# Placing the q/k projections of a recurrent-plus-MoE kernel inside its shared-expert loop

## The reference, cut to what matters

```python
q = xn @ Wq + bq;  k = xn @ Wk + bk;  v = xn @ Wv + bv     # 256 -> 256 each
logits = xn @ gate_w.T                                      # 16 experts, top 4, weights
# per expert: gather its tokens, silu(gate) * up, down; scatter-add with the weights
```

## Time and profile before

| what | value |
|---|---|
| median of 3 runs | 2452.93 us (2451.85 to 2453.05) |
| profiled execution, its own time | 2453.34 us |
| span of its profile | 2451.6 us |
| instructions in the profile | 38962 |
| `middle`, by the timeline | from about 1620 us to 1871 us |
| PE busy over the span | 2187.4 us (89%) |
| DVE, ACT, POOL busy | 1847.8, 1154.6, 1224.6 us |

### The profile page before, as it was taken

How to read it: one execution, slowest core, us unless ns; L and a number is a source line. 1 busy time by engine, 2 the same in 40 slices (tenths; PEclk the granted TensorE clock), 3 DMA queues, 4 the chain that set the end, 5 groups by cost and what they waited for, 6 DMA issues and landing times. The chain is left out here.

```text
span 2451.6 us, 38962 instructions
## 1 busy us (share of the span) xinstructions
PE 2187.4 (89%) x12914; PEld 1686.0 (69%) x12914; DVE 1847.8 (75%) x3389; ACT 1154.6 (47%) x2420; POOL 1224.6 (50%) x1324
## 2 busy tenths in 40 slices
PE   4995899999999999999999999968857998899982
PEld 3784688888888888888888888847755776344432
DVE  4885788888888888888888888744943444888746
ACT  1332455555555555555555555523333333366660
POOL 3544266565665665665656655533224332999000
PEclk9997699999999999999999999978988999799996
DMA  2002000000000000000000000043024555333214
GB/s 93 1 14 76 32 3 3 33 3 32 4 3 33 3 3 33 3 3 33 3 33 3 3 3 3 3 154 138 1 66 142 175 176 146 110 121 120 78 59 161
DMA packets 76743, 128.90 MB, mean 53 GB/s; under 512 B 22315, under 2 KB 54539, under 8 KB 74539
## 3 DMA queue, kind: packets, MB, share of 16 engines
q1 hardware_dynamic: 69584, 104.76, 12.5%
q0 software_dynamic: 6864, 18.75, 3.1%
q10 hardware_dynamic: 99, 2.88, 0.6%
HBM read 91.82 MB, written 46.92 MB: 57 GB/s over the span
## 5 line engine op out<-in xcount | busy, mean ns | idle before, releaser
L957 DVE SCALAR_TENSOR_TENSOR mix_cv<-mix_pp,mix_cw,mix_cv 128x384 f32<-128x384 f32 (+4 forms) x864 | 492.7, 570 | 25.4 <-ACT mix_cv L880 4.6
L804 PEld LDWEIGHTS mix_pyd<-mix_xdt,mix_lm 128*128 128x128 f32 x2048 | 248.4, 192 | 56.8 <-issue 53.1
L880 ACT ACTIVATE mix_cv<-mix_pp,mix_cb,mix_cw 128x384 f32<-128x384 f32 (+1 forms) x288 | 182.4, 633 | 205.1 <-PE mix_pp L80 205.1
L78 PE MATMUL mix_pp<-l0in_XH,mix_wx_lo 128*128 128x384 f32 (+2 forms) x576 | 239.1, 415 | 40.4 <-DVE mix_ss L946 25.4
L743 POOL TENSOR_TENSOR mix_xdt<-mix_xtok,l_dt 128x512 f32<-128x512 f32 x128 | 133.8, 1045 | 279.1 <-ACT mix_xtok L907 279.1
L736 POOL TENSOR_TENSOR mix_t<-mix_t,mix_xd 128x512 f32<-128x512 f32 x112 | 144.5, 1290 | 218.8 <-DVE mix_t L971 155.3
L855 PE MATMUL mix_pgt<-mix_wo,mix_gt 128*128 128x256 f32 x1024 | 246.4, 384 | 2.9 <-issue 2.2
L804 PE MATMUL mix_pyd<-mix_xdt,mix_lm 128*128 128x64 f32 x2048 | 243.7, 272 | 2.6 <-DVE mix_lm L1007 2.6
L1897 DVE TENSOR_REDUCE att_tops<-att_psc 128x1 f32<-128x512 f32 (+3 forms) x384 | 189.5, 549 | 47.3 <-PE att_psc L1845 32.2
L886 ACT ACTIVATE mix_pp<-mix_cv 128x384 f32<-128x384 f32 (+1 forms) x288 | 132.9, 462 | 161.7 <-DVE mix_cv L957 159.4
L855 PEld LDWEIGHTS mix_pgt<-mix_wo,mix_gt 128*128 128x128 f32 x1024 | 185.0, 191 | 31.5 <-issue 9.2
(11 more groups left out here) (382 smaller groups left out, 5817.5 us busy)
## 6 DMA issues: line engine op xcount, KB each, us to landing
mix_w_raw<-in_w_in SPq DMA_DIRECT2D x8, 1280.0 KB, 6.0
y_d<-exp_ys SPq DMA_DIRECT2D x79, 128.0 KB, 1.7
a_part<-att_sums SPq DMA_DIRECT2D x32, 256.0 KB, 5.0
mix_ll<-cs SPq DMA_DIRECT2D x384, 4.0 KB
q<-q SPq DMA_DIRECT2D x12, 512.0 KB, 4.5
k<-k SPq DMA_DIRECT2D x12, 512.0 KB, 4.5
att_qs<-q SPq DMA_DIRECT2D x32, 192.0 KB
att_ks<-k SPq DMA_DIRECT2D x32, 192.0 KB
```

The source lines that it names most:

```text
L78: pe.matmul(out, l_lo, r_hi, start=start, stop=False)
L804: last = pe.matmul(pyd[:, h * HP:(h + 1) * HP], lm[p % 2][:, h, :], xdt[p % 2][:, h * HP:(h + 1) * HP], start=True, stop=True)
L880: act.activation(conv_tile(k), pp[k % 2][:, halo:cols], ACT.Identity, bias=cb[:, it // 2, ct:ct + 1], scale=cw[:, it // 2, ct, 3:4]).then_ ...
L957: last = dve.scalar_tensor_tensor(out, of, cw[:, g, ct, 3 - d:4 - d], out, ALU.mult, ALU.add)
```

## The change

It moves the 16 q/k units into the loop over the shared expert's units. At n = 9 to 24 PE does, after the gate and up products of n, the projection of u = n-9, into the one bank `px`, and then the down product of n-2. The rest of unit u follows: high part on ACT at iteration n, after `hh`; DVE's subtraction at the head of iteration n+1; middle part (ACT) and low part (POOL) at n+1. The loops of ACT, DVE and POOL get the two more iterations that PE's has. Before the projection of u PE waits for DVE's subtraction of u-1.

The other parts: the output bank `po` is emptied behind `hh` of the same iteration (m = n-2, where it was m = n-3 ahead of it); token transposes, normalisations, logits, the prefix and the casts come one iteration later; q/k/v weights get buffers of their own and are split at n = 4 to 7; 28 matmuls of identity on identity are put ahead of PE's first transpose; the one-hot tables are made by 8 `tensor_tensor` compares of 16 columns' worth each (16x128 or 16x80 elements) in place of 128 `tensor_scalar` ones; `same` and `val` are made in two halves in one buffer, and the inversion is 32 matmuls at the head of n = 23 and 32 at the head of n = 25, summed in bank `pr`; the v tiles come after the loop, in banks `pg[0]` and `pu[0]`; the down weights are loaded by SP after the last q/k store has landed, and `experts` waits for them at its first down product (`w2_ld`); the table `keep` is loaded on its own.

```diff
-        DONE_AT = (0,) * 9 + (3, 9, 15, 21, 27, 32, 39, 42, 48, 50, 52, 54, 56, 57, 60, 60, 60) + (62,) * 14
-        PREFIX_AT, IDX_AT = 15, 2
+        TURN_AT = {4: 2, 5: 3, 6: 4, 7: 5, 8: 6, 9: 7}
+        NORM_AT = {3: 1, 5: 2, 7: 3}
+        LOGIT_AT = {0: 0, 6: 1, 8: 2, 10: 3}
+        DONE_AT = (0,) * 10 + (3, 9, 15, 21, 27, 32, 39, 42, 48, 50, 52, 54, 55, 57, 58, 61)
+        PREFIX_AT, IDX_AT = 16, (23, 25)
+        QK_AT, WARM = 9, 28
...
+                for a, sem in enumerate(stored):
+                    sp.wait_ge(sem, 16 * len(range(a, 16, NR3)))
+                sp.wait_ge(h_done, NU)
+                sp.wait_ge(idx_done, 2)
+                sp.wait_ge(dv, 61)
+                sp.dma_start(W[0:EI // 2, WG_COLS:], wd_d).then_inc(w2_ld, 16)
...
+                def third(u):
+                    pool.wait_ge(p1_done, u + 1)
+                    pool.tensor_tensor(part[u % NR3][:, 2, :], r, part[u % NR3][:, 1, :], ALU.subtract).then_inc(p2_done, 1)
...
+                def invert(half):
+                    pe.wait_ge(dv, (55, 58)[half])
+                    pe.wait_ge(val_done, half + 1)
+                    for j in range(NH2):
+                        last = pe.matmul(pr[:, 0:2 * TILE_COLS], opos[:, half * NH2 + j, :], val[:, j, :, :].rearrange("p v q -> p (v q)"),
+                                         start=half == 0 and j == 0, stop=half == 1 and j == NH2 - 1)
+                    last.then_inc(idx_done, 1)
...
+                for _ in range(WARM):
+                    pe.matmul(px[:, 0:P], ident[:, :], ident[:, :], start=True, stop=True)
...
+                    if n in IDX_AT:
+                        invert(IDX_AT.index(n))
...
                         last.then_inc(gu_done, 1)
+                    if 0 <= n - QK_AT < len(QK):
+                        project(n - QK_AT)
                     m = n - LAG
...
+                def second(u):
+                    act.wait_ge(sub1, u + 1)
+                    act.activation(part[u % NR3][:, 1, :], r, ACT.Copy).then_inc(p1_done, 1)
...
+                    if QK_AT < n:
+                        second(n - QK_AT - 1)
...
+                        act.wait_ge(h_done, n + 1)
+                        wait(act, out_done, n - NH + 1)
+                        act.activation(hh[n % NH][:, :], h[n % 2][:, :], ACT.Copy).then_inc(hh_done, 1)
+                    if 0 <= n - QK_AT < len(QK):
+                        u = n - QK_AT
+                        act.wait_ge(mm, u + 1)
+                        wait(act, stored[u % NR3], 16 * (u // NR3))
+                        col = u // 8 * 2 + u // 4 % 2
+                        act.activation(part[u % NR3][:, 0, :], px[:, :], ACT.Identity, bias=bq[:, col:col + 1]).then_inc(p0_done, 1)
+                    m = n - LAG
                     if m >= 0 and m % NS == NS - 1:
...
+                    if n in (22, 24):
+                        half = n // 2 - 11
+                        act.wait_ge(dv, (54, 57)[half])
+                        wait(act, idx_done, half)
+                        for t in range(NT // 2):
+                            last = act.activation(val[:, 4 * t:4 * t + 4, 0, :], same[:, 4 * t:4 * t + 4, :], ACT.Copy,
+                                                  scale=float(half * NT // 2 + t))
                         last.then_inc(val_done, 1)
...
-                        for i in range((j - 48) * 16, (j - 47) * 16):
-                            last = dve.tensor_scalar(opos[:, i, :], iota[:, :], posf[:, i:i + 1], None, ALU.is_equal)
+                        at = slice((j - 48) * 16, (j - 47) * 16)
+                        last = dve.tensor_tensor(opos[:, at, :], posf[:, at].unsqueeze(2).to_broadcast([P, 16, P]),
+                                                 iota[:, :].unsqueeze(1).to_broadcast([P, 16, P]), ALU.is_equal)
...
+                for n in range(NU + LAG):
+                    if QK_AT < n:
+                        u = n - QK_AT - 1
+                        dve.wait_ge(p0_done, u + 1)
+                        wait(dve, p2_done, u)
+                        col = u // 8 * 2 + u // 4 % 2
+                        dve.scalar_tensor_tensor(r, px[:, :], bq[:, col:col + 1], part[u % NR3][:, 0, :],
+                                                 ALU.add, ALU.subtract).then_inc(sub1, 1)
...
+                dispatch(61)
+                dispatch(62)
+                dve.wait_ge(dv, 63)
...
-                        pe.wait_ge(w_ld, 32)
+                        pe.wait_ge(w_ld, 16)
...
+                        if e == 0:
+                            pe.wait_ge(w2_ld, 16)
```

More of the change, by code:

```diff
@@ L1064, in middle @@
[L1064 to L1068, removed]
@@ L1069, in middle, with at @@
-        before = W[0:1, B:B + SLOTS1 * E].rearrange("p (j e) -> p j e", e=E)
+        def at(a, n):
+            return W[:, B + a:B + a + n]
+        raw = at(0, 3072).rearrange("p (i b k n) -> p i b k n", i=NS, b=2, k=KD)
+        draw = at(3072, 1536).rearrange("p (i n) -> p i n", i=NS)
+        oh = at(0, 1024).rearrange("p (t k e) -> p t k e", t=NT, k=TOPK)
+        big = at(1024, 1024).rearrange("p (t k e) -> p t k e", t=NT, k=TOPK)
+        cnt, inc, base = (at(1024 + i * 256, 256).rearrange("p (e t) -> p e t", e=E) for i in range(3))
@@ new lines, in middle @@
+        lg, cur, aux = (at(2048 + i * 256, 256).rearrange("p (t e) -> p t e", e=E) for i in range(3))
+        keep = at(2816, 256)
+        mb = at(3072, 128).bitcast(BF16).rearrange("p (t e) -> p t e", e=E)
+        slotf = at(3200, 64)
+        tileu, posu = (at(3264 + i * 64, 64).bitcast(U32) for i in range(2))
+        tilef, posf = keyb[:, 0, :], keyb[:, 1, :]
+        NH2 = NPAIR // 2
+        same = at(0, 1280).bitcast(BF16).rearrange("p (j q) -> p j q", j=NH2)
+        val = at(1280, 2560).bitcast(BF16).rearrange("p (j v q) -> p j v q", j=NH2, v=2)
@@ L1071, in middle @@
+        before = W[0:1, B:B + SLOTS1 * E].rearrange("p (j e) -> p j e", e=E)
+        wq = at(4608, 1536).rearrange("p (k n) -> p k n", k=KD)
+        trif = at(6656, 256)
+        part = [at(4352 + o * 768, 768).bitcast(BF16).rearrange("p (k t) -> p k t", k=3) for o in range(NR3)]
+        r = at(6656, TB)
+        th = [at(7168 + a * TB, TB) for a in range(2)]
         XN = VN[:, 0:NT * D].rearrange("p (t d) -> p t d", t=NT)
@@ L1466, in dispatch @@
                         dve.wait_ge(pfx_done, 1)
+                        dve.wait_ge(k_ld, 16)
                         last = dve.tensor_copy(cnt, pr[:, 256:512].rearrange("p (t e) -> p e t", e=E))
                     elif j == 33:
-                        last = dve.tensor_tensor_scan(inc.rearrange("p e t -> p (e t)"), table(C_KEEP, 256),
+                        last = dve.tensor_tensor_scan(inc.rearrange("p e t -> p (e t)"), keep,
                                                       cnt.rearrange("p e t -> p (e t)"), 0.0, ALU.mult, ALU.add)
@@ L1550, in _ @@
                 tokens_lo(1)
-                for n in range(NU):
-                    o = n % 2
-                    dve.wait_ge(th_done, n + 1)
-                    wait(dve, hl_done, n - 1)
-                    dve.scalar_tensor_tensor(h[o][:, :], th[o][:, :], 1.0, pg[o][:, :], ALU.add, ALU.mult).then_inc(s_done, 1)
-                    dve.wait_ge(s_done, n + 1)
-                    dve.tensor_tensor(h[o][:, :], h[o][:, :], pu[o][:, :], ALU.mult).then_inc(h_done, 1)
-                    extra(n)
@@ new lines, in _ @@
+                dispatch(61)
+                dispatch(62)
+                dve.wait_ge(dv, 63)
+                dve.memset(V[:, :, :, DH:], 1.0).then_inc(ones_set, 1)
+                dve.wait_ge(ones_set, 1)
+                for t in range(NT):
+                    dve.wait_ge(mv, t + 1)
+                    kt, side = t % (NT // 2), t // (NT // 2)
+                    dve.tensor_tensor(V[:, side * H1:(side + 1) * H1, kt, 0:DH], pv[t % 2][:, 0:D].rearrange("p (h c) -> p h c", h=H1),
+                                      bvs[:, :].rearrange("p (h c) -> p h c", h=H1), ALU.add).then_inc(vs, 1)
@@ L2131, in lay_out @@
     moe[:, C_PCOL] = np.arange(P)
-    moe[:, C_KEEP:C_KEEP + E * NT] = (np.arange(E * NT) % NT != 0)
+    keep = np.tile((np.arange(E * NT) % NT != 0).astype(np.float32), (P, 1))
     moe[:, C_ONES:C_ONES + E] = 1
```

219 lines of the change are left out of this document (79 added, 140 removed).

## The result

The changed kernel takes 2422.69 us (median of 4 runs, 2420.62 to 2423.21) against 2452.54 for the kernel before beside it: ratio 0.9876, 95% interval 0.9863 to 0.989. That is 29.9 us less. The prediction was 2423.0, in a range of 2410 to 2437. The profiled execution took 2423.18 us for a span of 2421.4; the profile of before has 2451.6, so the two spans are 30.2 us apart.

What follows compares the result with a forecast made beforehand. PE was taken to idle under DVE's one-hots and behind q/k stores held by the down weights' load. Gains 12.0 (early units) + 20.9 (unit 9 on) - 2.5 (handover) = 30.4 us gave 2423, range 2410 to 2437.

Steps and rivals of the forecast that it cites:

- the handover: From the last v add to the experts: the first gather may wait for the down weights' load, 2.5 us lost (0 to 4.5).
- the warm matmuls: Ahead of PE's first transpose: 28 matmuls lift the clock for the first logits and unit 0, 3.9 us gained (0 to 4.7).
- First nine units: Start of `middle` up to unit 9: 12.0 us gained in sum, ends 5 and 16.
- The two waits for transposes: In the first nine units: transposes one unit later find their rows ready, 5.4 us gained, plus 3.3 for a half-clock stretch.
- The output bank: In the first nine units: emptied right behind the down product, not behind the next tanh, 1.9 us gained.
- POOL's sixth low part: In the first nine units: the sixth weight slice's low part, needed by unit 5, comes late, 2.5 us lost (1 to 4).
- Unit 9 to the end of the last v add: Second stretch of `middle`: 109.1 us of PE's work plus 24.4 and 3 makes 136.5, a gain of 20.9 (10 to 32).
- the rounds: From unit 9 on: `dispatch` rounds and later scalar steps on DVE delay the next projections, 6 us of waits.
- the one-hots: From unit 9 on: DVE's compares for the one-hot tables make units late, 7.7 us of waits.
- the rival for more gain: Compares take half their price (-6) and the early part gives its 16 (-4): 2412 us, chance 0.15.
- the slower one: Compares on broadcast tables cost 5.8 ns an element, a loss of 58 us in all: 2481 us, chance 0.04.
- The rival of warm matmuls that don't lift the clock: Early part of `middle`: the clock isn't lifted where it matters, 3.9 us less gain, 2427 us, chance 0.08.

Runs made afterwards that it cites:

- experiment 3: The changed kernel without its 28 warm matmuls (`WARM = 0`): 2422.04 us, ratio 0.9875.
- experiment 10: The kernel before, q/k projections still behind the loop, with shifted early tables, the 8 compares and the down weights' load after the q/k stores in 8 DMAs: 2428.38 us.
- experiment 7: The changed kernel with the first half of the inversion at the head of iteration 24 in place of 23: 2417.0 us, ratio 0.9854.
- experiment 4: The changed kernel with the down weights' load cut into 8 DMAs of 4 KB rows, at the same place: 2419.02 us, ratio 0.9853.

## Why the prediction was right

Right as a whole, and most waits came where it had put them, but with errors that cancelled: that the sum is right to 0.3 us is luck. The step that failed by most is the handover, with the warm matmuls next to it. By its steps:

- **First nine units: 12.0 predicted, 11.9 measured, of other pieces.** (1) The warm matmuls, 3.9: failed. They gave 0 (experiment 3), since the clock fell again in the wait before the first transpose, the lower end that the prediction had named and not taken. (2) The two waits for transposes, 5.4, are gone, and the half-clock stretch of 3.3 is gone too. The windows from 17 us after the start of `middle` to unit 9, before and then after, have the granted clock third from the end:

```profile
1637.07:1712.24 75.17, 62.10 (x307) 53.74 (x307) 32.84 (x65) 22.82 (x45) 26.75 (x24) 0.81 0.43 158
```

```profile
1633.86:1697.15 63.29, 55.89 (x282) 48.37 (x283) 31.22 (x62) 23.03 (x45) 28.29 (x25) 0.82 0.50 186
```

With only two levels, full and half, 75.17 x 0.19 x 2 = 29 us and 63.29 x 0.18 x 2 = 23 us passed at the lower one: 6 us less, or 3 us of PE's time. (3) The output bank, 1.9: gone. (4) POOL's sixth low part, 2.5: 1.6. What made up for the warm matmuls is a term that was put at nothing: a block of logits, from 1709.64 to 1712.24 in the kernel before, stood ahead of unit 9's gate product and stands behind it now.

```profile
1709.64 0.17 PE L78 MATMUL mid_pr<-mid_wrh,l_XL 128*128 128x18 f32 x1
```

The prediction counted these 2.7 us in the second stretch and did not take them off the first. 5.4 + 3 + 1.9 - 1.6 + 2.6 = 11.3 of 11.9.
- **Unit 9 to the end of the last v add: 136.5 predicted, 137.0 measured** (136.6 to its start). The waits were over-priced: in the rounds 4.5 (four of 0.75, 0.54, 0.97), not 6; the one-hots 5.7, not 7.7; 4.3 at unit 23 and 2.9 in iteration 24 as named; 1.2 in iteration 25, not 2.4. They are 18.6 us in all, against 23.0 for the same terms. The clock was under-priced: the windows of 47 and 19 us have a mean granted clock of 0.89 and 0.81, so 47 x 0.11 x 2 = 10 and 19 x 0.19 x 2 = 7 us of them passed at the lower level, half of full speed. With 109.1 of PE's own work, 137.0 - 109.1 - 18.6 = 9.3 us are left for it and for small gaps, where 3 and 1.4 had been set.
- **The compares.** 2.28 us for 2048 elements, 1.49 for 1280, as worked out by the element; 3.27 us at most beside POOL, whose subtraction then took 1.98 us in place of 1.30. 2.3, 1.5 and up to 3.6 had been written. The Trainium skill (SBUF — State Buffer, Who interferes with whom) has the two exclude each other. The trace agrees: POOL's subtraction began 1.44 us into a first compare of 2.28, with 0.84 of it to go, and took 0.7 us longer than alone; the next compare began 1.1 us before that subtraction ended and took 1.0 longer than alone. The Trainium skill's rule on the step (VectorE: DVE Perf Modes, Mode 2×_1P) agrees too, with 1.1 ns an element: no speed-up. So neither half the price, the rival for more gain, nor 5.8 ns, the slower one, is borne out.
- **The handover: 2.5 predicted, 6.4 measured**, beyond its end of 4.5. This is the term that was mis-sized. Two numbers were off. The load's length was taken from a store that landed in 20.3 us, but the store went out behind the load; the windows of before show it until 1844, 23 us. And its start on the last v add was 11.1 us, not 12. So it ran 12 us past that add, not 8.
- **The signs.** Unit 9's gate product at 1697.15 (1700 written), the last v tile at 1834 (1836), waits of 0.75 to 0.97, of 2.9 and of 4.3 us as named, no wait for a store: borne out. (From the start of `middle` these are 80.3 and 217.3 us, where the written times make 79.9 and 215.9 by the start of before.) The first unit at full clock: not. Of the three signs that it is wrong none appeared: compares of 3.27 us at most, unit 9 before 1708, and a mean granted clock of 0.94 from unit 9 on, though 0.89 and 0.81 in two of its windows.
- **The total: 2423.0 predicted, 2422.7 measured.** In the profiled pair the kernel's own share of the 30.2 us is 27.0, the rest is the start of `middle`, which differs by up to 3.9 us between kernels. The rival of warm matmuls that don't lift the clock came true in its condition and not in its 2427. So the closeness is better than the working deserves; a miss of 3 us would have been as good a result.
- **Where the gain is from.** By single parts in the old order: the tables 7.3 us, the compares 9.6, the load's place by itself 0. The prediction had the projections fill PE's hole under DVE's one-hots, and the load behind the stores fill the other. The second is what the runs show. In the old order the load's move alone made the way to the last v add 17.9 us shorter and the compares alone 8.6, and with both and the tables PE got from unit 9 to that add in 130.5 us (experiment 10); the changed kernel needs 136.6, with 13.1 us of waits at the single bank and 5.5 for `val`, and a granted clock of 0.89 and 0.81 in the windows that hold the long ones. With the inversion later it is down to 130.5 too (experiment 7). So the projections' place did not shorten the way to the last v add. It let the stores, and with them the load, end sooner against the last v add, and so saved what the old order loses in the handover. The kernel of experiment 10 also lacks the output bank's earlier emptying and `keep`'s own load; what these give by themselves no run shows, but if they give something, the projections' place gives less.

## What to carry to other kernels

A large load moved away from one group of small transfers is moved onto another: before moving it, ask which transfers go out while it runs, and whether it can start its own length ahead of the first of them. Where it can't, cut its rows: 8 DMAs with 4 KB rows finished in 13 to 19 us where one with 32 KB rows took 23, and small transfers beside it landed in half the time (gathers 8.5 us for 16.4, a store 11.9 for 20.3). Work moved into another engine's holes is not a gain by itself: leave it in its old place in a kernel that has all the other parts, and see what is left. And where two profiles are compared by a mark, ask which work changed sides of it. Matmuls that only warm TensorE gave nothing here, since waits stood between them and the work; look for the clock in the window of the work, not in that of the warm matmuls.

## What the runs showed of the hardware that was not expected

- A load of 88 rows of 32 KB moved at 126 to 164 GB/s in the windows shown; in rows of 4 KB the same bytes moved at 230 to 265 in one profile and 173 to 217 in another. Over the whole load the busy share is near 0.70 in both (0.67 and 0.70). The Trainium skill (DMA: Bandwidth & Descriptors, Why a DMA increments its semaphore by 16 and not by 1) says that a DMA uses the largest number of engines up to 16 that divides its rows. By it, 88 rows go to 11 engines, an estimated share of 0.69. The trace agrees with 0.70 and 0.71 in the windows of experiment 4; no run tried another split.
- A gather beside this load landed after 16.4 us with long rows and 8.5 with short ones, 3 without it. The Trainium skill (same page, Queues, rings and completion order) has each DMA engine change between queues at packets. That the wait shrinks with the row fits (the number of DMAs changed with it); that it stays at 8.5 us with short rows shows that it is not all of it, and what the rest is stayed open.
- `middle` started at 1616.65 to 1620.52 us of the span in kernels whose code before it does the same work. A gain read off absolute times of two profiles can be wrong by that much. Times from the start of the phase agree to some tenths at unit 0 (its tanh at 25.9 to 26.4, and 27.2 once), but less so later: unit 9's tanh comes at 81.6 to 83.4 us in the seven kernels of the new order, whose code up to there is the same but for the warm matmuls.
